# A GNN stack on one core: who multiplies the summed paths by their coefficients, and the order of ScalarE's work in the last stage

## The chip, the cores and the metric

The kernel runs on one core of a Trainium2 chip. The metric is the time of one execution on the device in microseconds (us); lower is better. A core has TensorE (matmuls, "PE" in the profile, its weight loads "PEld"), VectorE ("DVE"), ScalarE ("ACT"), GpSimd ("POOL") and SyncE ("SP", which here issues DMAs). Each engine runs its own list of instructions in order, and they wait for one another by semaphores. A "q" behind an engine's name is its sequencer: it decodes, loads registers and waits, and hands instructions to the engine.

## The reference, cut to what matters

Four graph layers run one after another on 256 nodes x 512 features with 8192 edges: a 7-layer GENConv stack, a 4-block sparse attention stack, a mean-aggregating layer, and a segmented tensor product over edges. The change touches only the last one:

```python
# N_SEG = 16, EXTENT = 32, N_PATHS = 64; x_nodes: 256 x 512, x_edges: 8192 x 512
x1 = x_nodes[src].reshape(-1, N_SEG, EXTENT)
x2 = x_edges.reshape(-1, N_SEG, EXTENT)
i1, i2, i3 = (path_indices[:, 0], path_indices[:, 1], path_indices[:, 2])
contrib = path_coeffs[None, :, None] * x1[:, i1, :] * x2[:, i2, :]
edge_out = jnp.zeros((x2.shape[0], N_SEG, EXTENT)).at[:, i3, :].add(contrib)
out = jnp.zeros((n_nodes, OP_SIZE)).at[dst].add(edge_out.reshape(-1, OP_SIZE))
```

Each edge gets 64 "paths": segment `i1` of its source's features times segment `i2` of its own, times a coefficient, added into segment `i3` of the edge's result. The results are then summed over the edges of each destination node.

## The kernel before, in words

The 8192 edges are 64 tiles of 128. The last stage takes them in five groups of 10, 14, 14, 14 and 12 tiles (`SIZES`), so one VectorE instruction handles one path for a whole group: 128 partitions x (tiles x 32) elements, which is 320, 448 or 384 elements. The groups are called 0 to 4 here.

The 64 paths are treated in two ways.

- 44 of them (`SUMMED`) are "summed paths" or **rows**. For row r VectorE first forms a product with its coefficient into one of four slots of `prod` (line 1333, `scalar_tensor_tensor`: (source * coefficient) * edge), and later adds it into the group's `sums` at segment i3 (line 1323). The addition stands `AHEAD` = 2 rows behind the product, so the order is product r, addition r-1, product r+1, and so on. The slices are found by registers: `load_rows` (line 1317) loads the indices of up to four rows from SBUF into registers, on VectorE's sequencer. Each addition waits until the addition before it has ended, since both may write the same segment.
- 20 of them are five **sets** of four. VectorE forms their products without a coefficient (`set_rows`, line 1342) into `tail` and `prods` by turns, and TensorE sums them over destinations at once (`sum_set`, line 968) into its own accumulator. The coefficients come in at the end: ScalarE copies each accumulator out with its coefficient (line 729, `sums_out`), and TensorE spreads it to its segment (`spread_set`, line 976), for which ScalarE builds placing matrices (`place_rows`, lines 710 and 712).

VectorE's order in a group: set 0, a clearing of part of `sums`, rows 0 to 15, set 1, 7 rows, set 2, 7 rows, set 3, 7 rows, set 4, 7 rows, and the last two additions. `set_rows(s)` waits until TensorE has used the set two before it.

When a group's rows are done, TensorE adds its `sums` over destinations (`sum_group`, line 954) and then takes the next group's sets. Both need 0/1 matrices of destinations, which ScalarE builds with two activations for each tile (`hot`, lines 698 and 700: a square, then a Relu that waits for it). The matrix of a tile of group g goes to the place of that of group g-1, so it waits until TensorE has summed that tile. At the start of each group ScalarE and GpSimd also clear a part of `sums` (lines 704 and 541). In group 4 ScalarE builds the ten placing matrices first and the destination matrices after them.

In the last group TensorE takes set 0, set 1, spread 0, set 2, spread 1, set 3, spread 2, set 4, spread 3, spread 4, and then sums the group. The two additions to `x` (line 1357) and the store follow.

## Time and profile before

| | us |
|---|---|
| median of 3 runs | 954.59 (952.15 to 957.04) |
| the profiled execution: its own time | 958.74 |
| its span, first to last instruction | 956.9 |
| last stage, from VectorE's first set to the end of the span | 616.5 to 956.9 |

The span is some 2 us shorter than the time, since the time also holds what lies around the instructions. The page's shares are over the whole span; what counts here is the last stage, its last 340 us. A row of the timeline begins with the start and the duration of an instruction (or of several merged ones); what stands in brackets is how long the engine was idle before it and who ended that. Neighbouring instructions on an engine overlap a little, so the distance between two starts is shorter than the duration.

### The profile page before, as it was taken

Reading aid. Unit: us, or ns where it says so; the run is one execution under the profiler, and the core shown is the slowest. Engines: PE = TensorE matmul, PEld = TensorE weight load, DVE = VectorE, ACT = ScalarE, POOL = GpSimd, SP = SyncE. Lnnn points to the kernel's source line nnn. Section 1 sums busy time; section 2 is a strip of 40 time slices with the busy share of each in tenths; the row PEclk is TensorE's granted clock in tenths of the full one; section 3 lists DMA queues with packets and bytes.
Section 4 is the critical chain, followed back from the end, with each engine's and each line's share of the span. In section 5 each row is a group of like instructions: output and inputs, shape, how many; then the busy total and the mean of one; then the engine's idle time right before and its main releaser. Section 6 shows DMA issues by size and latency. Waiting matters only on the chain.

```text
span 956.9 us, 10169 instructions
## 1 busy us (share of the span) xinstructions
PE 784.0 (82%) x2802; PEld 500.9 (52%) x2802; DVE 608.1 (64%) x1562; ACT 226.7 (24%) x449; POOL 141.7 (15%) x153
## 2 busy tenths in 40 slices
PE   7287988978984999999999977126887998979998
PEld 3163554554552756766657543124465475565663
DVE  8463665655667353533543633178999999999980
ACT  6321120120221222222221311300420602406300
POOL 5000000000001000000010000720171081240000
PEclk9678999999996999999999999569998999999999
DMA  6703222322232224324333101820341344130000
GB/s 210 257 1 99 99 88 99 99 88 99 99 99 62 88 72 148 120 83 134 113 105 99 55 1 41 316 82 1 154 122 33 154 132 154 34 99 1 0 1 22
DMA packets 35905, 89.97 MB, mean 94 GB/s; under 512 B 3570, under 2 KB 3967, under 8 KB 35231
## 3 DMA queue, kind: packets, MB, share of 16 engines
q1 hardware_dynamic: 30752, 72.81, 22.0%
q0 software_dynamic: 5120, 16.78, 6.0%
q8 instruction: 13, 0.21, 0.1%
q14 instruction: 20, 0.16, 0.1%
HBM read 88.53 MB, written 1.05 MB: 94 GB/s over the span
## 4 chain that ended last, share of the span: by engine, by line
PE 35%; issue 29%; DVE 19%; DVEq 9%; SPq 3%; POOL 2%; DMA 2%; ACT 1%; POOLq 0%; ACTq 0%
PE PS L736 25%; DVE big L1323 6%; DVEq L1317 6%; PE PS L954 4%; DVE tail L1333 4%; PE PS L968 3%; POOL rstd L527 1%; DMA big<-_L_gnn_path_indices_dram 1%; DVE tail L1342 1%; DVE prods L1342 1%; DVEq L1323 1%; POOL big L547 1%; DVEq L1318 1%; PE PS L770 1%; DVE big L1096 1%
## 5 line engine op out<-in xcount | busy, mean ns | idle before, releaser
L1333 DVE SCALAR_TENSOR_TENSOR tail<-big,coef 128x448 f32 (+2 forms) x220 | 139.0, 634 | 1.5 <-issue 1.5
L736 PE MATMUL PS<-big 128*128 128x512 f32 (+1 forms) x368 | 136.2, 523 | 2.9 <-DVE big L1261 1.8
L1323 DVE TENSOR_TENSOR big<-big,tail 128x448 f32 (+2 forms) x220 | 127.0, 577 | 10.8 <-DVE tail L1333 5.1
L736 PEld LDWEIGHTS PS<-big 128*128 128x128 f32 x368 | 67.9, 190 | 65.8 <-issue 62.0
L527 POOL TENSOR_TENSOR rstd<-var,minus_half 128x1 f32<-128x1 f32 x38 | 28.7, 764 | 472.9 <-DVE var L1010 472.9
L547 POOL DMA_INDIRECT big<-h_rows,src_i x64 | 85.0, 1328 | 83.8 <-PE PS L954 60.6
L736 PE MATMUL PS<-hT,big 128*128 128x256 f32 x384 | 84.9, 381 | 4.2 <-ACT hT L648 4.2
L736 PEld LDWEIGHTS PS<-hT,big 128*128 128x128 f32 x384 | 72.3, 190 | 15.5 <-issue 3.9
L954 PE MATMUL PS<-big,hotd_more 128*128 128x512 f32 x176 | 76.3, 592 | 0.0
L1028 DVE TENSOR_TENSOR h<-PS,h 128x512 f32<-128x512 f32 x26 | 17.9, 689 | 79.7 <-PE PS L736 79.7
L968 PE MATMUL PS<-xn,tail 128*128 128x256 f32 x104 | 30.5, 445 | 40.8 <-issue 27.2
L704 ACT ACTIVATE big<-consts 128x3072 f32<-128x3072 f32 x5 | 13.8, 2762 | 201.3 <-DVE big L1323 187.2
L968 PE MATMUL PS<-xn,prods 128*128 128x256 f32 x96 | 31.2, 483 | 32.2 <-DVE prods L1342 32.2
L954 PEld LDWEIGHTS PS<-big,hotd_more 128*128 128x128 f32 x176 | 33.4, 190 | 42.1 <-issue 42.1
L968 PE MATMUL PS<-hotd_more,tail 128*128 128x256 f32 x224 | 54.3, 399 | 0.0
L968 PE MATMUL PS<-hotd_more,prods 128*128 128x256 f32 x216 | 51.6, 395 | 0.0
L736 PE MATMUL PS<-cnt,big 128*128 128x256 f32 x224 | 50.6, 385 | 0.0
L968 PEld LDWEIGHTS PS<-hotd_more,tail 128*128 128x128 f32 x224 | 46.0, 206 | 7.6
L968 PEld LDWEIGHTS PS<-hotd_more,prods 128*128 128x128 f32 x216 | 44.1, 204 | 7.2
L968 PEld LDWEIGHTS PS<-xn,tail 128*128 128x128 f32 x104 | 21.9, 216 | 49.0 <-issue 29.4
L736 PEld LDWEIGHTS PS<-cnt,big 128*128 128x128 f32 x224 | 42.9, 194 | 5.7
L736 PE MATMUL PS<-big,vhid 128*128 128x256 f32 x96 | 28.6, 464 | 18.5 <-DVE vhid L1125 18.5
(184 smaller groups left out, 1067.0 us busy)
## 6 DMA issues: line engine op xcount, KB each, us to landing
big<-in_L_gnn_vn_W_dram SPq DMA_DIRECT2D x12, 1024.0 KB, 5.3
big<-in_edge_attr_dram SPq DMA_DIRECT2D x3, 3584.0 KB, 10.7
big<-in_L_gnn_m_w_dram SPq DMA_DIRECT2D x8, 1024.0 KB, 5.3
big<-in_L_gnn_gcn_W_dram SPq DMA_DIRECT2D x7, 1024.0 KB, 5.3
big<-in_L_gnn_wv_dram SPq DMA_DIRECT2D x4, 1024.0 KB, 5.3
big<-in_L_gnn_wq_dram SPq DMA_DIRECT2D x4, 1024.0 KB, 5.2
big<-in_L_gnn_wk_dram SPq DMA_DIRECT2D x4, 1024.0 KB, 5.4
big<-in_L_gnn_wo_dram SPq DMA_DIRECT2D x4, 1024.0 KB, 5.4
```

Of the source, the lines that this page charges most:

```text
L527: pool.tensor_tensor(rstd[:, t:t + 1], var[:, t:t + 1], minus_half[:, t:t + 1], ALU.pow).then_inc(ln_est, 1)
L547: pool.indirect_dma_start(out=part[SOURCE_AT[g]][:, j, :], out_offset=None, in_=h_rows, in_offset=bass.IndirectOffsetOnAxis(ap=src_i[:, ti ...
L704: act.activation(cut, zero.to_broadcast([P, (ZERO_CUT[1] - ZERO_CUT[0]) * D]), ACT.Copy).then_inc(acc_zero, 1)
L736: return pe.matmul(o, lhsT, rhs, start=start, stop=stop)
L770: ins = pe.transpose(chunks(0)[:, c, t * P:(t + 1) * P], xn[:, t, c * P:(c + 1) * P], ident[:])
L954: ins = pe.matmul(PS[:, t, :], hotd(j)[:, t * P:(t + 1) * P], part[SUM_AT[g]][:, j, :], start=False, stop=True, skip_group_check=True)
L968: ins = pe.matmul(PS[:, 2 + s, 0:N], prods[n % 2][:, j, :], hotd(j), start=False, stop=True, skip_group_check=True)
L1028: link(dve.tensor_tensor(to[:, t, :], PS[:, bank + t, :], to[:, t, :], ALU.add))
L1317: dve.load([r for four in regs[0:n_rows] for r in four], path[0:1, row * 4:(row + n_rows) * 4])
L1323: dve.tensor_tensor(o, o, prod[:, row % RING, 0:n, :], ALU.add)._wait_ge(path_step, g * STEPS + 2 * row + 1).then_inc(path_step, 1)
L1333: dve.scalar_tensor_tensor(out=prod[:, row % RING, 0:n, :], in0=xs[:, :, bass.ds(i1, EXT)], scalar=coef[:, row:row + 1], in1=xe[:, :, bass ...
L1342: ins = dve.tensor_tensor(prods[(g * SETS + s) % 2][:, 0:n, q * EXT:(q + 1) * EXT], xs[:, :, bass.ds(i1, EXT)], xe[:, :, bass.ds(i2, EXT)] ...
```

## The change

VectorE's product of a row loses its coefficient: it becomes a plain `tensor_tensor` multiplication. ScalarE multiplies each product by its coefficient, in place in `prod` (`scale_row`). VectorE's addition of a row stands three rows behind its product now, and product r waits until ScalarE has scaled row r-2. Behind product 43 VectorE waits for the last scaling, loads registers, and makes three additions.

ScalarE's list in a group is laid out anew: clearing, then rows 0 to 43, each one scaling, with the building work spread among them by `built_by`: a "unit" (two activations: one destination matrix, or in group 4 also one placing matrix) after two of three rows, and two units more after rows 16, 23, 30 and 37, as long as there are units left (14 in groups 1 to 3, 22 in group 4, none in group 0, whose matrices are built before). In group 4 the first four copies of set sums stand behind rows 34, 35, 38 and 41. TensorE's spreads 0, 1 and 2 now stand together behind set 3.

```diff
-AHEAD = 2
+AHEAD = 3
+SUM_OUT_AFTER = (34, 35, 38, 41)
 # ScalarE
+            def scale_row(g, row):
+                act.wait_ge(path_step, g * STEPS + row + 1 + max(0, row - AHEAD + 1))
+                at = prod[:, row % RING, 0:SIZES[g], :]
+                act.activation(at, at, ACT.Copy, scale=coef[:, row:row + 1]).then_inc(scaled, 1)
+            def built_by(row):
+                return 2 * row // 3 + sum(2 for s in range(1, SETS) if row > SUMMED_FIRST + SUMMED_PER_SET * (s - 1))
...
-                if g == GROUPS - 1:
-                    act.wait_ge(negcol_set, 1)
-                    place_rows()
-                for j in range(SIZES[g]):
-                    act.wait_ge(tile_summed, min(START[g - 1] + j + 1, START[g]))
-                    hot(g, j)
+                for row in range(SUMMED):
+                    scale_row(g, row)
+                    for i in range(built_by(row), built_by(row + 1)):
+                        if g and i < SIZES[g]:
+                            act.wait_ge(tile_summed, min(START[g - 1] + i + 1, START[g]))
+                            hot(g, i)
+                        if last and SIZES[g] <= i < SIZES[g] + 2 * SETS:
+                            place_row(i - SIZES[g])
+                    if last and row in SUM_OUT_AFTER:
+                        sum_out(SUM_OUT_AFTER.index(row))
+            sum_out(SETS - 1)
 # TensorE
                     sum_set(g, s)
-                    if g == GROUPS - 1 and s:
-                        spread_set(s - 1)
+                    if g == GROUPS - 1 and s == SETS - 2:
+                        for early in range(SETS - 2):
+                            spread_set(early)
+            spread_set(SETS - 2)
             spread_set(SETS - 1)
 # VectorE
                     dve.tensor_tensor(o, o, prod[:, row % RING, 0:n, :], ALU.add)._wait_ge(
-                        path_step, g * STEPS + 2 * row + 1).then_inc(path_step, 1)
+                        path_step, g * STEPS + min(2 * row + AHEAD - 1, SUMMED + row)).then_inc(path_step, 1)
...
-                                dve.scalar_tensor_tensor(
-                                    out=prod[:, row % RING, 0:n, :], in0=xs[:, :, bass.ds(i1, EXT)],
-                                    scalar=coef[:, row:row + 1], in1=xe[:, :, bass.ds(i2, EXT)],
-                                    op0=ALU.mult, op1=ALU.mult).then_inc(path_step, 1)
+                                ins = dve.tensor_tensor(prod[:, row % RING, 0:n, :], xs[:, :, bass.ds(i1, EXT)],
+                                                        xe[:, :, bass.ds(i2, EXT)], ALU.mult)
+                                if row >= AHEAD - 1:
+                                    ins._wait_ge(scaled, g * SUMMED + row - (AHEAD - 2))
+                                ins.then_inc(path_step, 1)
...
+                dve.wait_ge(scaled, (g + 1) * SUMMED)
                 summed_rows(SUMMED, SUMMED + AHEAD)
```

Three places show the new order. First ScalarE in group 4, where before all units stood in one run (L710 and L712 build a placing matrix, L698 and L700 a destination matrix; xn and hotd_more hold the latter):

```order
L704 ACTIVATE big<-consts 128x3072 [waits path_step]
L710 ACTIVATE big<-iota_f,negcol 128x256 [waits negcol_set]
L712 ACTIVATE big<-big,consts 128x256 [waits place_squared]
L710 ACTIVATE big<-iota_f,negcol 128x256
L712 ACTIVATE big<-big,consts 128x256 [waits place_squared]
...
L698 ACTIVATE xn<-iota_f,dst_n 128x256 [waits tile_summed]
L700 ACTIVATE xn<-xn,consts 128x256 [waits hot_squared]
...
L729 ACTIVATE big<-PS,setcoef 128x256 [waits set_used] x5
```

Now, in the same group, from row 14's scaling to row 17's and the unit behind it (L718 is a scaling, L700 and L702 a destination matrix, L711 and L713 a placing matrix):

```order
L718 ACTIVATE tail<-tail,coef 128x384 [waits path_step]
L700 ACTIVATE hotd_more<-iota_f,dst_n 128x256 [waits tile_summed]
L702 ACTIVATE hotd_more<-hotd_more,consts 128x256 [waits hot_squared]
L718 ACTIVATE tail<-tail,coef 128x384 [waits path_step] x2
L700 ACTIVATE hotd_more<-iota_f,dst_n 128x256 [waits tile_summed]
L702 ACTIVATE hotd_more<-hotd_more,consts 128x256 [waits hot_squared]
L700 ACTIVATE hotd_more<-iota_f,dst_n 128x256 [waits tile_summed]
L702 ACTIVATE hotd_more<-hotd_more,consts 128x256 [waits hot_squared]
L711 ACTIVATE big<-iota_f,negcol 128x256
L713 ACTIVATE big<-big,consts 128x256 [waits place_squared]
L718 ACTIVATE tail<-tail,coef 128x384 [waits path_step]
L711 ACTIVATE big<-iota_f,negcol 128x256
```

The "x2" are the scalings of rows 15 and 16; three units stand between the scalings of rows 16 and 17. Groups 1 to 3 have the same order there.

Second, TensorE in group 4 behind set 2, before (L968 sums a set; a second row of it per set, without `set_ready`, is left out; L976 spreads, L954 sums the group):

```order
L968 MATMUL PS<-xn,prods 128x256 [waits hotd_ready,set_ready]
...
L976 MATMUL PS<-big 128x512 [waits sums_out,place_ready]
L976 MATMUL PS<-big 128x512
L968 MATMUL PS<-xn,tail 128x256 [waits hotd_ready,set_ready]
...
L976 MATMUL PS<-big 128x512 [waits sums_out,place_ready]
L976 MATMUL PS<-big 128x512
L976 MATMUL PS<-big 128x512 [waits sums_out,place_ready]
L976 MATMUL PS<-big 128x512
L954 MATMUL PS<-big,xn 128x512 [waits path_step]
```

And now (L988, L996 and L974 are the same three):

```order
L988 MATMUL PS<-xn,prods 128x256 [waits hotd_ready,set_ready]
...
L996 MATMUL PS<-big 128x512 [waits sums_out,place_ready]
L996 MATMUL PS<-big 128x512
L996 MATMUL PS<-big 128x512 [waits sums_out,place_ready]
L996 MATMUL PS<-big 128x512
L996 MATMUL PS<-big 128x512 [waits sums_out,place_ready]
L996 MATMUL PS<-big 128x512
L988 MATMUL PS<-xn,tail 128x256 [waits hotd_ready,set_ready]
```

Between set 3 and set 4 there was one spread (number 2, the first L976 pair shown); now there are three, numbers 0, 1 and 2.

Third, the end of a group on VectorE, before (L1333 is a product, L1323 an addition, L1317 the register load, the ISA rows register arithmetic):

```order
L1323 TENSOR_TENSOR big<-big,tail 128x12x32 [waits path_step]
L1333 ISA
L1333 SCALAR_TENSOR_TENSOR tail<-big,coef 128x384
L1317 TENSOR_LOAD path
L1318 ISA
L1323 TENSOR_TENSOR big<-big,tail 128x12x32 [waits path_step]
L1323 ISA
L1323 TENSOR_TENSOR big<-big,tail 128x12x32 [waits path_step]
```

And now (L1357 is a product, L1345 an addition, L1339 the register load):

```order
L1345 TENSOR_TENSOR big<-big,tail 128x12x32 [waits path_step]
L1357 ISA
L1357 TENSOR_TENSOR tail<-big 128x384 [waits scaled]
L1339 TENSOR_LOAD path [waits scaled]
L1340 ISA
L1345 TENSOR_TENSOR big<-big,tail 128x12x32 [waits path_step]
L1345 ISA
L1345 TENSOR_TENSOR big<-big,tail 128x12x32 [waits path_step]
L1345 ISA
L1345 TENSOR_TENSOR big<-big,tail 128x12x32 [waits path_step]
```

The last register load now waits for ScalarE, and three additions stand behind it where there were two.

## Rows read from the trace of the kernel before

**Rows 1.** Windows, group 1 and group 4: length, busy times, clock.

```profile
core 0: us, PE busy (x) PEld busy (x) DVE busy (x) ACT busy (x) POOL busy (x), PEclk, DMA share, GB/s
676.00:741.00 65.00, 55.38 (x181) 38.07 (x182) 62.45 (x110) 16.74 (x30) 24.14 (x16) 0.89 0.34 114
870.00:932.00 62.00, 60.02 (x196) 38.13 (x196) 55.38 (x109) 24.83 (x50) 1.57 (x1) 0.97 0.00 1
```

**Rows 2.** Timeline, VectorE, group 1: rows in steady state.

```profile
683.51 0.62 DVE L1323 TENSOR_TENSOR big<-big,tail 128x448 f32 x1
684.04 0.68 DVE L1333 SCALAR_TENSOR_TENSOR tail<-big,coef 128x448 f32 x1
684.64 0.62 DVE L1323 TENSOR_TENSOR big<-big,tail 128x448 f32 x1
685.77 0.62 DVE L1323 TENSOR_TENSOR big<-big,tail 128x448 f32 x1
687.00 0.62 DVE L1323 TENSOR_TENSOR big<-big,tail 128x448 f32 x1
```

**Rows 3.** Timeline, start of group 1 and its product 19.

```profile
676.33 2.76 ACT L704 ACTIVATE big<-consts 128x3072 f32<-128x3072 f32 x1 [68.59 <-DVE big L1323]
677.50 2.23 DVE L1342 TENSOR_TENSOR prods<-big 128x448 f32 x4 [1.21 <-issue]
680.73 1.15 DVE L1333 SCALAR_TENSOR_TENSOR tail<-big,coef 128x448 f32 x2
704.67 0.67 DVE L1333 SCALAR_TENSOR_TENSOR tail<-big,coef 128x448 f32 x1
```

**Rows 4.** Timeline, end of group 3 on VectorE, start of group 4.

```profile
867.83 0.68 DVE L1333 SCALAR_TENSOR_TENSOR tail<-big,coef 128x448 f32 x1
868.42 1.28 DVE L1323 TENSOR_TENSOR big<-big,tail 128x448 f32 x2
870.77 1.97 DVE L1342 TENSOR_TENSOR tail<-big 128x384 f32 x4 [1.06 <-issue]
873.72 1.02 DVE L1333 SCALAR_TENSOR_TENSOR tail<-big,coef 128x384 f32 x2
```

**Rows 5.** Groups of instructions from 600 us on: busy us, mean ns of one.

```profile
L1333 DVE SCALAR_TENSOR_TENSOR tail<-big,coef 128x448 f32 x132 | 88.6, 673 | 0.0
L1342 DVE TENSOR_TENSOR prods<-big 128x448 f32 x32 | 17.9, 620 | 3.1 <-issue 2.7
```

**Rows 6.** One group of ScalarE's instructions, whole span.

```profile
L623 ACT ACTIVATE big<-big,consts 128x512 f32<-128x512 f32 x14 | 10.1, 723 | 0.5
```

**Rows 7.** Timeline, ScalarE in group 4: one unit and the next one's start.

```profile
882.75 0.49 ACT L698 ACTIVATE xn<-iota_f,dst_n 128x256 f32<-128x256 f32 x1
883.27 0.51 ACT L700 ACTIVATE xn<-xn,consts 128x256 f32<-128x256 f32 x1
883.68 0.49 ACT L698 ACTIVATE xn<-iota_f,dst_n 128x256 f32<-128x256 f32 x1
```

**Rows 8.** Register loads of line 1317: ns, least, median, most.

```profile
L1317 DVEq TENSOR_LOAD <-path x95: 594/1097/1354, 614.7 to 927.6; - x95
```

**Rows 9.** Timeline, group 4: VectorE's sets and rows, TensorE to the end.

```profile
910.20 1.96 DVE L1342 TENSOR_TENSOR prods<-big 128x384 f32 x4 [0.26 <-issue]
918.05 1.88 PE L976 MATMUL PS<-big 128*128 128x512 f32 x4
919.88 1.96 DVE L1342 TENSOR_TENSOR tail<-big 128x384 f32 x4 [0.26 <-issue]
921.90 2.65 PE L968 MATMUL PS<-xn,tail 128*128 128x256 f32 x8 [1.98 <-DVE tail L1342]
939.17 13.90 PE L954 MATMUL PS<-big,hotd_more 128*128 128x512 f32 x32
953.11 1.29 DVE L1357 TENSOR_TENSOR x<-PS,x 128x512 f32<-128x512 f32 x2 [23.08 <-PE PS L954]
```

**Rows 10.** Windows around TensorE's idle time before set 4.

```profile
922.00:929.00 7.00, 7.00 (x25) 5.87 (x26) 7.00 (x15) 0.00 (x0) 0.00 (x0) 0.76 0.00 0
```

41 lines of the change are left out of this document (22 added, 19 removed).

## The prediction, made before the changed kernel was run

> **What bounds the kernel now.** I read the windows by group first. In groups 1 to 3 VectorE is busy in nearly all of the time (62.45 of 65.00 us in group 1) and TensorE has room; in group 4 TensorE is the full one, 60.02 of 62.00 us, VectorE 55.38 [rows 1]. So up to group 4 a group lasts as long as VectorE takes, and from there the end is set by when TensorE can take set 4: it stands idle for 1.98 us until VectorE has formed it, at 921.84, and from 921.90 it works without a pause up to the last additions at 953.11, 31.2 us later [rows 9]. Nothing before the last stage is touched.
>
> Next, VectorE's steady state. From an addition to the product behind it it is 0.53 us, from the product to the next addition 0.60, so a row takes 1.13; where a register load stands between, additions are 1.23 apart (685.77 to 687.00) [rows 2]. The load itself takes up to 1.10 us on the sequencer [rows 8], so it is hidden but for 0.1, because the sequencer runs about one row ahead. It can't run further, since an addition isn't handed over before the last one has ended: the two additions with nothing between take 1.28 us together, 0.66 apart [rows 4].
>
> ScalarE works for 16.74 us of group 1's 65 [rows 1], so it has room on average. What counts is whether it has it when VectorE waits.
>
> **What is removed.** A product with coefficient takes 673 ns, a plain one of the same 448 elements 620 [rows 5], and four plain ones take 2.23 us, that is 0.54 from start to start [rows 3]. So a product goes from 0.60 to 0.535 on VectorE: 0.065 a row, 44 x 0.065 = 2.9 us in a group, if nothing else paces the row. Behind a register load the load does, so I count two thirds.
>
> **What a scaling costs.** The trace before has no in-place scaling of 448 elements. The nearest rows are the activations from SBUF to SBUF: 0.51 us for 256 elements [rows 7] and 723 ns for 512 [rows 6]; these are the ends of my range. Between them 448 elements give 0.67 us, 384 give 0.62, 320 give 0.56; I take these, since both rows have, as the scaling does, a per-partition operand. Consecutive activations start 0.10 earlier than the last one ends (0.51 long, 0.41 to the next start) [rows 7]. So ScalarE spends 0.57 us a row in groups 1 to 3 and 0.52 in group 4. A unit (square, Relu) takes 0.93 to 0.94 us [rows 7]. The Trainium skill ("ScalarE: Activation LUTs", What ACT_TABLE_LOAD costs) puts an activation at 186 ns, 93 ns more for each per-partition operand and 0.833 ns an element; that is 0.65 us for the scaling, 0.02 less than mine, and by it the sum below would come out at about 976 us; no row here shows which is nearer.
>
> **Rows 0 to 19 of groups 1 to 3.** With a unit behind two rows of three ScalarE needs 0.57 + 0.67 x 0.94 = 1.20 us a row, VectorE only 1.07. Product r waits for scaling r-2, so VectorE can be only two rows ahead. Behind row 16 three units stand in one block, 2.8 us. They follow set 1, in whose 2.23 us ScalarE has nothing to do. Adding up ScalarE's time from the group's start: product 0 starts after 4.4 us (680.73 less 676.33) [rows 3], scaling 0 at 5.1; 18 scalings x 0.57 = 10.3; 13 units x 0.94 = 12.2; idle in set 1 2.2. Scaling 17 ends at 29.8, and product 19, which waits for it, starts at 29.9. Before it started at 704.67, 28.3 after the start [rows 3]: **+1.6 us**. The register load for row 20 stands behind this waiting product and can't be hidden: some 1.4 us with its register arithmetic, of which 0.53 to 1.0 lie beside the product: **+0.7**. ScalarE's wait for `tile_summed` costs nothing here: TensorE needs 1.7 us a tile (32 matmul instructions in 13.90 us, four a tile) [rows 9], ScalarE's units come every 1.8, and later.
>
> **Rows 20 to 43**: 24 x 0.065 = 1.6, two thirds of it: **-1.0**. ScalarE has no units left there, 0.57 against 1.07, so it hides.
>
> **The end of a group.** Before: product 43 starts at 867.83, the last addition ends at 869.70, so 1.87 us [rows 4]. Now: product 0.62, hand-over to ScalarE 0.06 (as TensorE's behind set 4 [rows 9]), scaling 0.67, hand-over 0.06, then the register load and its arithmetic, 1.1 (VectorE's 1.06 us of idle time at a group's start, where it waits for just that [rows 4]), and three additions 0.66 + 0.66 + 0.62. That is 4.45: **+2.6**. Queued behind are the next group's set 0 and TensorE's `sum_group`; both move by it.
>
> Together a group of 14 tiles has 1.6 + 0.7 - 1.0 + 2.6 = +3.9; three of them **+11.7 us**. Group 0 has no units; its rows are shorter than the loads (two plain operations of 320 elements against a load of 1.10 every four rows plus arithmetic), so I count a third of 44 x 0.06, -0.9, and +2.5 for its end: **+1.6**.
>
> **Group 4, up to set 4.** 22 units now, three more at each set. Product 0 comes after 4.0 us [rows 4], so scaling 0 at 4.6. Up to scaling 27: 28 x 0.52 = 14.6, 21 units x 0.94 = 19.7, idle in sets 1 and 2 3.9: 42.8. Product 29 waits for it, then the load (1.4) and set 3 (1.96) and the product itself (0.5) follow: set 3 ends at 46.7 at least, 47.2 with half of the exposed loads. Before it ended at 912.16, 42.4 after 869.73 [rows 4, 9]: +4.8. From there to the end of set 4 it is as long as before (9.7). Set 4 comes **+4.8** later.
>
> **TensorE's new order.** Set 4 stands behind spreads 0, 1 and 2 now, and spread 2 needs the copy that ScalarE makes behind scaling 38, while product 38 stands behind set 4 on VectorE. From the end of set 4: to the start of product 38 1.5, product 0.55, hand-over 0.06, scaling 0.62, copy 0.06 + 0.47 + 0.06, spread 1.7 (1.88 busy [rows 9]): TensorE starts set 4 5.0 us after VectorE has it, where it was 0.06 before: **+4.9**. Set 4, spreads 3 and 4 and the last group then take their 31.2 us as before. VectorE's last addition (seven rows and the longer end, 11 us behind set 4) lies beside TensorE's 15.
>
> **Sum:** 11.7 + 1.6 + 4.8 + 4.9 = 23.0. Against the profiled execution, 958.74, that is 981.7. The median of the runs is 4.15 below that one, so **977.6, say 978 us**. With scalings of 0.51 us some 10 would go (18 x 0.16 less in each of three groups, 28 x 0.11 in the last, of which VectorE's own pace keeps some): 968. With 0.723: 18 x 0.05 x 3 + 28 x 0.1 = 5.5 more: 983. These bound the likeliest case.
>
> **Rivals.**
> (A) Slower still, by the clock: TensorE's idle time lowers it. Behind 1.98 us of idle time the window of set 4 has a mean granted clock of 0.76, a mix of the two levels 1.2 and 2.4 GHz [rows 9, 10]. Now its idle times before sets 3 and 4 are longer. If set 4 ran at the low level throughout, its 24 instructions would take twice 0.216 each, 10.3 us for the 7.0 of before, and spread 2 as much again as it has, 1.7: +5. With long scalings that is 985 to 988. The Trainium skill ("TensorE: Matmul & The Clock Gate", HAM oscillation) says just this: work in bursts with idle gaps between starts cold each time. By it alone the sum would be 983. Against it: the three spreads fill part of the gap.
> (B) ScalarE's work is covered. If a scaling took under 0.44 us of its time (1.07 less 0.63 for units), VectorE would never wait in the rows. Left are the product's gain, -1.9 in a group, -0.5 for a product moved ahead of the first addition, and the end, +2.6: +0.2 x 3; group 0 +1.6; group 4 -2.0 and +4.9. Sum +5.1: 960. For it: on average ScalarE is idle for 48 of 65 us [rows 1]. Against it: 0.51 us for 256 elements.
> (C) Faster: three rows of distance let the sequencer run ahead, and the register loads vanish from VectorE's path. Then groups 1 to 3 get the full 2.9 and 1.0 of load stalls, and the last load is read ahead of its wait, so the end costs only 1.2: -2.7 x 3; group 0 -4 (it has the most load stalls); group 4 -1: -13, 942. It decides at the point where a waiting product no longer stops its sequencer. Against it: additions still wait one for another [rows 4], and the load is a sequencer instruction behind the wait.
> (D) The change doesn't do what it says: a plain product is no quicker here. Against it are 132 and 32 instructions of one shape [rows 5]. It would add 44 x 0.065 x 2/3 x 4 = 7.6: 985.
>
> **How the numbers follow.** Forecast 0.64; A 0.12; B 0.14; C 0.06; D 0.04. I take 0.5% (4.8 us) as what a measurement of this kernel tells from no change. B lies on that edge, half of it on either side. Slower: 0.64 + 0.12 + 0.04 + 0.07 = 0.87; same 0.07; faster 0.06. The range goes from 963, between B and the lower end of the forecast, to 990, with A and D in it.
>
> **What would show it.** Product 19 of group 1 some 30 us behind the group's start, with a wait for ScalarE, and products 17 and 18 without one. At each end of a group some 2.6 us between product 43 and the first of three additions. Groups 1 to 3 lasting 68 us instead of 64 to 65. In group 4 TensorE waiting for ScalarE's copy before spread 2. A scaling of 0.62 to 0.70 us for 448 elements. I am wrong if VectorE's products don't wait for ScalarE behind row 16, if the end of a group is under 3 us, or if TensorE takes set 4 at once.

## The result, and the profile after

| | before | after |
|---|---|---|
| median of 4 runs each, us | 953.87 (952.15 to 957.04) | 975.72 (971.93 to 978.36) |
| span of the profiled execution, us | 956.9 | 974.1 |

The changed kernel takes 1.0222 times as long, with a 95% interval of 1.0178 to 1.0266. The forecast was 978 us, slower; it came out slower, at 975.7.

The lines are L1357 for a product, L1345 for an addition, L1367 for a set's product and L718 for a scaling. By form, from 600 us on (columns: busy us, mean ns | idle before, releaser), in a second profile of the changed kernel:

```profile
L718 ACT ACTIVATE tail<-tail,coef 128x448 f32<-128x448 f32 x132 | 86.0, 662 | 64.9 <-DVE tail L1357 64.9
L1345 DVE TENSOR_TENSOR big<-big,tail 128x448 f32 x132 | 81.9, 620 | 13.2 <-DVE tail L1357 7.2 <-issue 5.8
L1357 DVE TENSOR_TENSOR tail<-big 128x448 f32 x132 | 81.3, 618 | 4.9 <-ACT tail L718 4.9
L718 ACT ACTIVATE tail<-tail,coef 128x384 f32<-128x384 f32 x44 | 25.9, 606 | 14.9 <-DVE tail L1357 14.9
```

A product went from 673 to 618 ns [rows 5] (forecast: 620). A scaling takes 662 ns for 448 elements and 606 for 384 (forecast: 670 and 620). An addition still takes 620 ns, so VectorE's own instructions don't get longer with ScalarE scaling beside them. The change does what it says.

The waits of the last stage in the first profile (us in total, times, longest):

```profile
DVE big L1345 <- DVE tail L1357: 13.9, 24, 1.0
DVE big L1345 <- issue: 11.1, 10, 1.9
DVE tail L1357 <- ACT tail L718: 8.8, 10, 1.7
```

Of 220 products only 10 show a wait for ScalarE. The additions lost more than the products: a register load that isn't ready in time shows as idle time before the addition that stands behind it. In the kernel before, these idle times come to 5.1 us in 10 places, here to 13.9 in 24. Most of them stand behind products that show no wait themselves. In group 1 (scaling 5, product 7 and the addition behind it):

```profile
684.75 0.65 ACT L718 ACTIVATE tail<-tail,coef 128x448 f32<-128x448 f32 x1
685.68 0.62 DVE L1357 TENSOR_TENSOR tail<-big 128x448 f32 x1
686.98 0.63 DVE L1345 TENSOR_TENSOR big<-big,tail 128x448 f32 x1 [0.68 <-DVE tail L1357]
```

Product 7 may start when scaling 5 has ended, at 685.40. That is early enough for the engine, which gets to product 7 at 685.68, but VectorE's sequencer hadn't been able to pass the wait and load the registers of the next four rows before. The same happens at product 11; the version below without any scaling has no idle time at these two places. In group 1 the additions lose 2.4 us in this way, in four places, where they lost 0.5 before.

The timeline of VectorE at product 19 of group 1, which answers to [rows 3]; the group starts at 674.07:

```profile
701.47 0.62 DVE L1357 TENSOR_TENSOR tail<-big 128x448 f32 x1
702.01 0.62 DVE L1345 TENSOR_TENSOR big<-big,tail 128x448 f32 x1
704.06 0.62 DVE L1357 TENSOR_TENSOR tail<-big 128x448 f32 x1 [1.44 <-ACT tail L718]
705.32 0.63 DVE L1345 TENSOR_TENSOR big<-big,tail 128x448 f32 x1 [0.63 <-DVE tail L1357]
705.86 0.62 DVE L1357 TENSOR_TENSOR tail<-big 128x448 f32 x1
```

And ScalarE in the same stretch (L700 and L702 are the two activations of a unit):

```profile
699.98 0.67 ACT L718 ACTIVATE tail<-tail,coef 128x448 f32<-128x448 f32 x1 [2.00 <-DVE tail L1357]
700.56 0.49 ACT L700 ACTIVATE hotd_more<-iota_f,dst_n 128x256 f32<-128x256 f32 x1
701.08 0.51 ACT L702 ACTIVATE hotd_more<-hotd_more,consts 128x256 f32<-128x256 f32 x1
...
702.96 0.51 ACT L702 ACTIVATE hotd_more<-hotd_more,consts 128x256 f32<-128x256 f32 x1
703.38 0.65 ACT L718 ACTIVATE tail<-tail,coef 128x448 f32<-128x448 f32 x1
```

Product 19 starts 0.03 us after scaling 17 ends (703.38 + 0.65). Between scalings 16 and 17 stand the three units, from 700.56 to 703.47. Just before, while VectorE formed set 1, ScalarE was idle for 2.00 us. So it was not short of time; its work stood in the wrong place. The addition behind product 19 starts 1.26 us after it, where the steady distance is 0.53, again because of a register load.

The end of group 3, which answers to [rows 4]:

```profile
874.49 0.62 DVE L1357 TENSOR_TENSOR tail<-big 128x448 f32 x1
877.00 1.94 DVE L1345 TENSOR_TENSOR big<-big,tail 128x448 f32 x3 [1.89 <-issue]
880.01 1.97 DVE L1367 TENSOR_TENSOR tail<-big 128x384 f32 x4 [1.07 <-issue]
```

From product 43 to the end of the last addition it is 4.45 us, where it was 1.87. The 1.89 us hold the wait for the last scaling and the load behind it. They are put down to "issue", not to ScalarE, since the wait is an instruction of the sequencer.

TensorE, from the sum of group 3 (L974) through group 4's sets (L988) and spreads (L996); it answers to [rows 9]:

```profile
878.99 9.73 PE L974 MATMUL PS<-big,xn 128*128 128x512 f32 x16 [3.58 <-DVE big L1345]
...
926.74 3.78 PE L988 MATMUL PS<-xn,prods 128*128 128x256 f32 x8 [5.31 <-DVE prods L1367]
930.32 4.47 PE L988 MATMUL PS<-hotd_more,prods 128*128 128x256 f32 x16
934.63 3.60 PE L996 MATMUL PS<-big 128*128 128x512 f32 x8
939.08 1.95 PE L996 MATMUL PS<-big 128*128 128x512 f32 x4 [0.86 <-ACT big L722]
940.87 1.89 PE L988 MATMUL PS<-xn,tail 128*128 128x256 f32 x8
942.60 3.62 PE L988 MATMUL PS<-hotd_more,tail 128*128 128x256 f32 x16
```

TensorE takes set 4 at 940.87, 61.9 us after the group's start at 878.94; before it was 52.2. It also shows two things that the forecast didn't count: 16 matmuls of the sum take 9.73 us where they took 7.13 before, and set 3 takes 8.05 us (926.74 to 934.79) where a set at full clock takes 5.35 (set 4, 940.87 to 946.22). The windows beside these rows (the column PEclk is the mean granted clock; 1.00 is 2.4 GHz and 0.50 is 1.2):

```profile
core 0: us, PE busy (x) PEld busy (x) DVE busy (x) ACT busy (x) POOL busy (x), PEclk, DMA share, GB/s
926.00:935.00 9.00, 8.43 (x25) 6.84 (x26) 8.49 (x19) 4.95 (x9) 0.00 (x0) 0.65 0.01 3
935.00:973.00 38.00, 34.43 (x92) 17.02 (x90) 10.45 (x21) 5.42 (x10) 0.00 (x0) 1.00 0.04 13
```

These two are from the second profile of the changed kernel, whose set 3 starts at 926.58. At set 3 the clock is mostly at the lower level, and behind it at the full one.

### A comparison that misled at first

By the first two profiles group 0 had become 4.4 us faster (59.7 to 55.4), against a forecast of +1.6. In the first profile of the kernel before, VectorE stood still in group 0 for reasons that no engine's work explains:

```profile
627.14 0.49 DVE L1323 TENSOR_TENSOR big<-big,tail 128x320 f32 x1 [2.70 <-issue]
```

In that stretch the register instructions of VectorE's sequencer take 0.70 us each, where the median is 0.08, while GpSimd issues its gathers. A second profile of each kernel, both on one chip, tells whether the change has to do with it.

> The kernel before again, for group 0 alone. In its first profile some register instructions of VectorE's sequencer took 0.70 us each in group 0, and the group 59.8 us; in the changed kernel there were none and it took 55.4. Theory (it belongs to the execution or the chip, not to the kernel; kernels of one later call had such instructions and those of an earlier call none): the two kernels of this call agree, both with or both without. Rival (the changed order avoids them): before2 has them and lasts about 60 us, after2 none and 55.

> The changed kernel again, for group 0 alone, on the same chip as before2. Theory (execution or chip): as before2, with or without the 0.70 us register instructions, and if with them group 0 lasts about 60 us. Rival (the changed order avoids them): none, and 55 us.

The kernel before took 957.5 us (span 955.7) and the changed one 975.75 (span 973.9), and neither had those long instructions (the longest of L1333 and L1357 takes 0.10 us), though GpSimd issues the same gathers; the same stretch before reads:

```profile
626.89 0.49 DVE L1323 TENSOR_TENSOR big<-big,tail 128x320 f32 x1
627.30 0.55 DVE L1333 SCALAR_TENSOR_TENSOR tail<-big,coef 128x320 f32 x1
```

The same kernel shows them in one execution and not in another, so they are no work of the change. In the profiles of the experiments they were there for all kernels that ran on a chip together, or for none. The medians of the kernel before on these chips fit: 957.99 and 956.75 us where the profiles have them, 953.96 and 954.73 where they have not. What causes them stays open. So between chips the ratios are compared and not the times, and this pair of profiles is the one to compare. A group's length is from the end of its predecessor's last addition to the end of its own; group 4's is to the end of the span:

| us | group 0 | 1 | 2 | 3 | 4 and end | last stage |
|---|---|---|---|---|---|---|
| before, second profile | 54.1 | 64.5 | 64.1 | 64.9 | 87.2 | 334.9 |
| after, second profile | 55.4 | 68.2 | 68.0 | 68.6 | 94.6 | 354.8 |
| difference | +1.3 | +3.7 | +3.9 | +3.7 | +7.4 | +19.9 |
| forecast | +1.6 | +3.9 | +3.9 | +3.9 | +9.7 | +23.0 |

The spans of this pair differ by only 18.2 us, since the last stage starts at 620.81 before and at 619.08 after. Nothing ahead of it was changed; over all the profiles here that start lies between 615.4 and 620.8, so a single execution's time is uncertain by some us for reasons that have nothing to do with the change.

### The profile page after: what moved, and what is told of

Same layout as the page of the kernel before. It is cut to its first block, busy times and chain, and to the rows that moved or that the text cites. A ratio compares the mean times of both kernels' runs of the same rounds, so it can differ in the third digit from the quotient of the medians.

```text
span 974.1 us, 10395 instructions
## 1 busy us (share of the span) xinstructions
PE 791.6 (81%) x2802; PEld 504.2 (52%) x2802; DVE 597.3 (61%) x1562; ACT 353.9 (36%) x669; POOL 127.9 (13%) x153
## 4 chain that ended last, share of the span: by engine, by line
PE 37%; issue 27%; DVE 16%; DVEq 7%; ACT 6%; SPq 3%; POOL 2%; DMA 2%; POOLq 0%; ACTq 0%
PE PS L756 26%; PE PS L974 5%; DVEq L1339 5%; DVE big L1345 5%; PE PS L988 4%; DVE tail L1357 4%; ACT tail L718 2%; POOL rstd L529 1%; DMA big<-_L_gnn_path_indices_dram 1%; DVE tail L1367 1%; DVE prods L1367 1%; DVEq L1340 1%; POOL big L549 1%; PE PS L790 1%; PE PS L846 1%
## 5 line engine op out<-in xcount | busy, mean ns | idle before, releaser
L718 ACT ACTIVATE tail<-tail,coef 128x448 f32<-128x448 f32 (+2 forms) x220 | 136.6, 631 | 116.7 <-DVE tail L1357 116.6
L1345 DVE TENSOR_TENSOR big<-big,tail 128x448 f32 (+2 forms) x220 | 127.7, 580 | 25.7 <-DVE tail L1357 13.9
L1357 DVE TENSOR_TENSOR tail<-big 128x448 f32 (+2 forms) x220 | 126.7, 578 | 8.8 <-ACT tail L718 8.8
L756 PEld LDWEIGHTS PS<-big 128*128 128x128 f32 x368 | 67.9, 190 | 65.9 <-issue 62.0
L549 POOL DMA_INDIRECT big<-h_rows,src_i x64 | 71.2, 1112 | 87.5 <-PE PS L974 64.3
L974 PE MATMUL PS<-big,hotd_more 128*128 128x512 f32 x176 | 76.3, 592 | 0.0
L988 PE MATMUL PS<-xn,tail 128*128 128x256 f32 x104 | 29.4, 432 | 39.2 <-DVE tail L1367 39.2
L988 PE MATMUL PS<-hotd_more,prods 128*128 128x256 f32 x216 | 52.8, 397 | 5.5 <-ACT hotd_more L702 5.5
L988 PE MATMUL PS<-xn,prods 128*128 128x256 f32 x96 | 31.4, 485 | 29.8 <-DVE prods L1367 29.8
L974 PEld LDWEIGHTS PS<-big,hotd_more 128*128 128x128 f32 x176 | 33.4, 190 | 42.1 <-issue 42.1
L974 PE MATMUL PS<-big,xn 128*128 128x512 f32 x80 | 43.6, 707 | 14.0 <-DVE big L1345 14.0
L988 PE MATMUL PS<-hotd_more,tail 128*128 128x256 f32 x224 | 52.2, 388 | 0.0
L988 PEld LDWEIGHTS PS<-hotd_more,prods 128*128 128x128 f32 x216 | 42.5, 200 | 14.3 <-ACT hotd_more L702 8.3
L756 PE MATMUL PS<-big,vhid 128*128 128x256 f32 x96 | 34.3, 536 | 18.6 <-DVE vhid L1147 18.6
L988 PEld LDWEIGHTS PS<-hotd_more,tail 128*128 128x128 f32 x224 | 44.1, 197 | 6.6
L988 PEld LDWEIGHTS PS<-xn,tail 128*128 128x128 f32 x104 | 22.0, 217 | 46.7 <-DVE tail L1367 42.1
```

Source lines behind the costliest of these rows:

```text
L549: pool.indirect_dma_start(out=part[SOURCE_AT[g]][:, j, :], out_offset=None, in_=h_rows, in_offset=bass.IndirectOffsetOnAxis(ap=src_i[:, ti ...
L718: act.activation(at, at, ACT.Copy, scale=coef[:, row:row + 1]).then_inc(scaled, 1)
L756: return pe.matmul(o, lhsT, rhs, start=start, stop=stop)
L974: ins = pe.matmul(PS[:, t, :], hotd(j)[:, t * P:(t + 1) * P], part[SUM_AT[g]][:, j, :], start=False, stop=True, skip_group_check=True)
L988: ins = pe.matmul(PS[:, 2 + s, 0:N], prods[n % 2][:, j, :], hotd(j), start=False, stop=True, skip_group_check=True)
L1345: dve.tensor_tensor(o, o, prod[:, row % RING, 0:n, :], ALU.add)._wait_ge(path_step, g * STEPS + min(2 * row + AHEAD - 1, SUMMED + row)).th ...
```

## The experiments

All ratios are to the kernel before, run on the same chip, with a 95% interval. Group lengths are from the profiles.

### One cost at a time: the units moved

```diff
-  ... sum(2 for s in range(1, SETS) if row > SUMMED_FIRST + SUMMED_PER_SET * (s - 1))
+  ... sum(2 for s in range(1, SETS) if row >= SUMMED_FIRST + SUMMED_PER_SET * (s - 1))
```

The block of extra units now stands behind row 15, that is beside set 1 on VectorE, and likewise one row earlier at the other sets.

> The two extra units stand behind the scalings of rows 15, 22, 29 and 36 instead of 16, 23, 30 and 37, so ScalarE builds them while VectorE forms a set. Theory (the block of units holds back scaling 17, and product 19 behind it): product 19 of groups 1 to 3 starts some 28 us behind the group's start instead of 29.8 to 30.1, these groups last about 66 us instead of 68, set 4 of group 4 ends at about 52.5 us instead of 57.0, and the whole is 8 to 11 us faster than the changed kernel. Rival (the scalings slow VectorE whatever the order, by traffic or by ScalarE's total work): groups 1 to 3 stay at 68 us and the whole within 2 us.

Measured: 969.06 us, ratio 1.0164 (1.0133 to 1.0194). Groups 1 to 3 last 66.3, 67.1 and 66.7. VectorE at product 19 of group 1 (the group starts at 672.95):

```profile
700.89 0.61 DVE L1345 TENSOR_TENSOR big<-big,tail 128x448 f32 x1
701.42 0.61 DVE L1357 TENSOR_TENSOR tail<-big 128x448 f32 x1
702.31 0.62 DVE L1345 TENSOR_TENSOR big<-big,tail 128x448 f32 x1 [0.27 <-DVE tail L1357]
```

Product 19 starts at 28.5, where it was before the change, and shows no wait; the load behind it costs 0.27 instead of 0.63. The mechanism is as forecast. The idle time before additions hardly fell, though: 12.6 us in all instead of 13.9, since the exposed loads of rows 0 to 15 are still there. The whole gained 6.7 us (the kernel before took 953.96 here and 953.87 beside the changed kernel), less than the 8 to 11 expected. Group 2 gave only 1.0, since there VectorE stood idle for 1.25 us before set 2 (it may take the place of set 0 only when TensorE has used that). Group 4 and the end gave 3.1 of it (92.1 instead of 95.2), since in group 4 VectorE's set 3 is still 2.3 us later than before the change and TensorE idles 3.43 us before it.

### One cost at a time: the end of a group

```diff
-                dve.wait_ge(scaled, (g + 1) * SUMMED)
-                summed_rows(SUMMED, SUMMED + AHEAD)
+                for k, (_, _, i3) in enumerate(load_rows(SUMMED, AHEAD)):
+                    if k:
+                        dve.wait_ge(scaled, (g + 1) * SUMMED - AHEAD + 1 + k)
+                    add_product(SUMMED - AHEAD + k, i3)
```

The registers are loaded first, and each addition waits for its own scaling.

> At a group's end the register load stands ahead of the wait, and additions 42 and 43 wait for scalings 42 and 43 each; addition 41 waits for none. Theory (the end costs 4.45 us because the load is serial with the wait for scaling 43): product 43 to the last addition's end falls to about 3.0 us, 1.4 less in each of groups 0 to 3; in group 4 it is hidden, so 5 to 6 us in all. Rival (the wait for the scaling alone costs it, the load is hidden): 4.1 to 4.4 us, under 1.5 us in all.

Measured: 969.5 us, ratio 1.0162 (1.0135 to 1.0189). The end of group 1:

```profile
732.97 0.61 DVE L1357 TENSOR_TENSOR tail<-big 128x448 f32 x1
733.50 1.93 DVE L1345 TENSOR_TENSOR big<-big,tail 128x448 f32 x3
```

The three additions follow with no gap: 2.47 us from product 43 to the end, instead of 4.45 (about 3.0 was expected). Groups 1 to 3 last 66.2, 65.9 and 66.7, each some 2 less. So 2.0 of the +2.6 at a group's end go with the order of load and waits, and 0.6 with the third addition. The edit does two things at once, and no run has them apart: the load stands ahead of the waits, and additions 41 and 42 no longer wait for scaling 43. By the terms of the forecast, an estimate, the first is worth 1.1 us and the second some 0.8.

### TensorE's new order in group 4: the copy, or the whole order?

```diff
-SUM_OUT_AFTER = (34, 35, 38, 41)
+SUM_OUT_AFTER = (34, 35, 36, 41)
```

This takes away only what the forecast names for the term: spread 2's wait for the copy behind scaling 38.

> Only the copy of set 2's sums stands behind row 36 instead of 38, ahead of set 4. By the prediction's term (TensorE gets set 4 4.9 us late because of spread 2's copy) the end would come some 3 to 5 us earlier. By the rival reading of the changed kernel's trace (TensorE waits only 0.86 us for that copy, the rest are spreads that it has to do anyway and that were kept out of its idle time before set 3) it comes about 1 us earlier.

Measured: 975.92 us, ratio 1.0227 (1.0199 to 1.0255); group 4 and the end 94.2, against 95.2. TensorE:

```profile
936.19 5.31 PE L996 MATMUL PS<-big 128*128 128x512 f32 x12
941.34 1.89 PE L988 MATMUL PS<-xn,tail 128*128 128x256 f32 x8
```

All three spreads run in one piece, and set 4 comes only 1.0 us earlier in the group than in the first profile of the changed kernel (60.9 after its start at 880.4), and 0.5 earlier than in the second (61.4). The copy was the last to come, but behind it TensorE was late by itself. The other version moves the spreads to where TensorE is idle, before set 3:

```diff
-SUM_OUT_AFTER = (34, 35, 38, 41)
+SUM_OUT_AFTER = (27, 28, 31, 41)
-                    if g == GROUPS - 1 and s == SETS - 2:
-                        for early in range(SETS - 2):
-                            spread_set(early)
+                    if g == GROUPS - 1 and s == SETS - 3:
+                        spread_set(0)
+                        spread_set(1)
+                    if g == GROUPS - 1 and s == SETS - 2:
+                        spread_set(2)
```

> Copies behind rows 27, 28, 31 and 41; TensorE takes spreads 0 and 1 behind set 2, spread 2 behind set 3. Theory (5.3 us of TensorE's idle time before set 3 are what group 4 loses, and set 3 then runs at a lower clock): spreads 0 and 1 lie in the idle time, set 3 runs at the full clock, TensorE starts set 4 within 0.2 us of its end on VectorE (57.0 us after the group's start, instead of 61.9), and the end comes 3 to 5 us earlier. Rival (VectorE's last addition or the clock sets the end): under 1.5 us.

Measured: 971.79 us, ratio 1.0195 (1.0163 to 1.0227); group 4 and the end 92.2, that is 3.0 and 2.4 less than in the two profiles of the changed kernel. TensorE:

```profile
921.02 3.67 PE L996 MATMUL PS<-big 128*128 128x512 f32 x8 [2.17 <-ACT big L722]
924.53 1.89 PE L988 MATMUL PS<-xn,prods 128*128 128x256 f32 x8
926.25 3.62 PE L988 MATMUL PS<-hotd_more,prods 128*128 128x256 f32 x16
929.71 1.88 PE L996 MATMUL PS<-big 128*128 128x512 f32 x4
933.36 1.99 PE L988 MATMUL PS<-xn,tail 128*128 128x256 f32 x8 [1.77 <-DVE tail L1369]
```

The gap of 5.31 us is mostly filled (2.17 are left), set 3 runs at full clock (5.34 us), and set 4 waits for VectorE again, as before the change. What is left of group 4's loss, 5.0 us, is as much as set 4 comes late on VectorE.

### All three together

> The three repairs together: units built beside the sets, the register load ahead of the last waits, copies and spreads in TensorE's idle time. Theory (three separate costs that add up): groups 1 to 3 last about 64.6 us (68.2 less 1.6 less 2.0), group 0 53.8, group 4 and the end about 85, so the time is about 947 us, some 1% under the kernel before, of which most is group 0. Rival (the costs hide one another, ScalarE's total work in rows 3 to 20 is the floor): groups 1 to 3 stay above 66 us and the time above 958.

Measured: 960.31 us against 957.99 for the kernel before on this chip, ratio 1.0031 (1.0011 to 1.0050). The 947 us expected were missed. Groups 1 to 3 came as expected, but group 4 and the end took 2 us more, and group 0 took 59.8 instead of 53.8: the expectation had compared with a kernel before that has the long register instructions, and not counted them here, where this profile has them too. In all, the last stage took 340.0 us where the expected lengths add up to 332.6; the other 6 us lie outside these lengths and stay unexplained.

Groups 1 to 3 last 64.3, 64.0 and 64.8, and group 4 and the end 87.1: each as before the change. So the three costs account for nearly all of the loss (0.3 of 2.2% is left), but the plain product gives nothing back even then. Rows 0 to 15 still take longer: from product 3 to product 15 of group 1 it is 14.9 us (6.8 to 21.7), against 13.8 before (7.8 to 21.5). ScalarE, with its units between the scalings, holds the waits of products 7 and 11 until shortly before they start, and the loads behind them stay exposed: 2.0 us of idle time before additions in this group, 0.5 before the change. The end of a group is 0.6 longer.

### Is it the length of a scaling?

```diff
-                act.activation(at, at, ACT.Copy, scale=coef[:, row:row + 1]).then_inc(scaled, 1)
+                act.activation(at, at, ACT.Copy, scale=2.0).then_inc(scaled, 1)
```

This kernel leaves the coefficients of the summed paths out of the result.

> The changed kernel with a constant 2.0 in place of the coefficient operand of the scaling; it leaves the coefficients of the summed paths out of the result. By the Trainium skill (ScalarE: Activation LUTs, What ACT_TABLE_LOAD costs) an activation is 93 ns shorter without a per-partition operand. Theory (ScalarE's own pace sets rows 3 to 19 and the sets of group 4): scalings of 448 elements take 0.56 to 0.58 us instead of 0.65 to 0.67, product 19 of groups 1 to 3 starts 1 to 1.7 us earlier, the whole is 5 to 8 us faster. Rival (the waits come from hand-over times, not from the scaling's length): under 2 us.

Measured: 977.34 us, ratio 1.0209 (1.0159 to 1.0258): no gain. Scalings did get shorter:

```profile
L718 ACT ACTIVATE tail<-tail 128x448 f32<-128x448 f32 x132 | 74.7, 572 | 74.2 <-DVE tail L1357 71.1 <-issue 2.5 <-DVE big L1345 0.6
```

572 ns instead of 662, and product 19 starts at 29.1, 28.9 and 29.2 instead of 30. The expectation failed all the same. In group 3 VectorE stands idle 1.3 us before set 2, because it waits until TensorE has used set 0. That is late, since TensorE's sum of group 2 starts slowly (27.3 us for the whole sum, 24.3 in the kernel before). There the wait moved from ScalarE to TensorE. Groups 1 to 3 last 67.2, 67.0 and 68.7, that is 1.0, 1.0 and -0.1 us less than in the changed kernel. These 2 us are within the spread of the runs (975.65 to 981.24). The wait of product 19 fell only from 1.44 to 1.25 us. The ratio, 1.0209 against 1.0222, says the same (the time itself holds the long register instructions, with 60.7 us for group 0). So 91 ns less for a scaling take away about a tenth of the loss at most.

### How much could the change give at all?

In the kernel before, only the product is made plain; the coefficients of the summed paths are left out.

```diff
-                                dve.scalar_tensor_tensor(..., scalar=coef[:, row:row + 1], ..., op0=ALU.mult, op1=ALU.mult)
+                                dve.tensor_tensor(..., ALU.mult)
```

> The kernel before with the plain product on VectorE and no scaling anywhere; it leaves the coefficients of the summed paths out. This is all that the change could give. Theory (0.065 us a row, a third of it lost behind register loads): groups 1 to 3 last 62.6 instead of 64.5 us, the whole is 7 to 10 us faster than before. Rival (the register loads pace the rows): under 3 us. Group 0: if its 4.4 us less in the changed kernel come with the plain product, it lasts 55 to 56 us here, otherwise 59.

Measured: 951.95 us, ratio 0.9939 (0.9910 to 0.9967), 6 us where 7 to 10 were expected. Groups 1 to 3 last 62.9, 62.8 and 63.5, some 1.4 less than before, where the forecast's share for this (two thirds of 2.9) is 1.9. So with ScalarE's part free, the plain product is worth 0.6%. That is the ceiling for the product. It isn't quite that of the whole change: the additions still stand two rows behind here. Three rows bring product 3 of group 1 forward, from 7.7 us after the group's start here to 6.8 in the changed kernel, and cost 0.6 at the group's end.

### TensorE's clock: kept busy before a sum

```diff
                     sum_set(g, s)
+                    if g < GROUPS - 1 and s == SETS - 1:
+                        keep_busy(7, 8)
```

Eight matmuls on an unused part of the accumulator (16 rows in the trace, two for each) fill the gap before each sum.

> The changed kernel with eight more matmuls (identity times a constant, into a bank that nobody reads) behind set 4 of groups 0 to 3, in TensorE's idle time of 3.5 us before each group's sum. Theory (that idle time lowers the granted clock, so that a sum of 14 tiles takes 27.0 us instead of 24.3): the sums take 24.3 to 24.6 us again, set 0 of group 4 ends 2.5 us earlier, and set 2 of group 4, which waits for it, comes 0.5 to 1.5 us earlier; groups 1 to 3 stay at 68 us, and the whole is 0 to 2 us faster. Rival (the slow sums hold VectorE in every group): groups 1 to 3 fall to 66 us or less.

Measured: 974.11 us, ratio 1.0210 (1.0173 to 1.0247). TensorE at the sum of group 3, to be read beside 878.99 above:

```profile
874.16 3.62 PE L756 MATMUL PS<-iota_f,ident 128*128 128x256 f32 x16
877.65 7.13 PE L974 MATMUL PS<-big,xn 128*128 128x512 f32 x16
```

The first 16 matmuls take 7.13 us in all three groups, instead of 9.73 to 9.91 in the first profile of the changed kernel. But groups 1 to 3 last as long as without this edit (68.2, 67.9, 68.6), and group 4 and the end take 94.7, against 95.2 and 94.6 in the two profiles of the changed kernel. The slow start of the sums is real; in the changed kernel as it is, at most some half a microsecond hangs on it.

### A version built on the findings

Rows 0 to 15 keep the coefficient on VectorE, ScalarE builds all units there and scales only rows 16 to 43; the end of a group is that of the second experiment, and TensorE has the order of before with `SUM_OUT_AFTER = (22, 28, 32, 41)`.

```diff
+OWN = SUMMED_FIRST
+                for j in range(SIZES[g]): hot(g, j)
+                for row in range(OWN, SUMMED): scale_row(g, row)
+                                if row < OWN: dve.scalar_tensor_tensor(...)
+                    if g == GROUPS - 1 and s:
+                        spread_set(s - 1)
```

> Rows 0 to 15 keep the coefficient in VectorE's product, as before the change; only rows 16 to 43 are scaled by ScalarE, which builds all its units first, as before. Copies behind rows 22, 28, 32 and 41, spreads in the old order behind each set, register load ahead of the last waits. Theory: no product waits for a unit; a group gains 28 rows x 0.065 x 2/3 = 1.2 us and 0.5 for the product ahead, and loses 0.6 at its end, so groups 1 to 3 last 63 to 63.8 us, and the whole takes 944 to 949 us. Rival (scalings in place slow VectorE's own instructions): groups 1 to 3 at 65 us or more.

Measured: 956.46 us, ratio 0.9980 (0.9952 to 1.0007): no difference from before, where 944 to 949 us were expected. As in the version with all three, group 0 has the long register instructions (59.1 us), which that expectation didn't count; this explains a part of the difference. Groups 1 to 3 last 62.7, 65.1 and 63.8, so groups 1 and 3 came as expected. In group 1 the idle time before additions is down to 0.2 us, from 2.0 with all three repairs: with no scaling in rows 0 to 15, the loads there are hidden again. Group 2 has a wait of its own (VectorE, us in total, times, longest; L1363 is a product here and L720 a scaling):

```profile
DVE tail L1363 <- ACT tail L720: 1.7, 1, 1.7
```

There ScalarE's last unit waited for TensorE's sum of group 1, whose first 16 matmuls took 8.83 us, and scaling 16 behind it came late. The same kernel with four matmuls to keep TensorE busy before each sum tests that:

> e8_mixed with four more matmuls into an unread bank behind set 4 of groups 0 to 3. In e8_mixed group 2 lasted 65.1 us, since product 18 waited 1.7 us for scaling 16, which stood behind a unit that waited for TensorE's sum, and that sum ran at a lower granted clock (26.0 us). Theory (the clock is what delays it): the sum of group 2 takes 24.3 us, the wait goes, group 2 lasts 63 to 63.5 us, and the whole is 0.4 to 0.8% faster than the kernel before. Rival (units paced by tile_summed hold scaling 16 whatever the clock): group 2 at 65 us, no difference from the kernel before.

Measured: 959.5 us, ratio 1.0027 (1.0002 to 1.0052). The wait is gone, and group 2 lasts 63.4 instead of 65.1, as expected; the whole is not faster, against the expectation. In the two profiles, which both have the long register instructions, the last stage is 1.2 us shorter with the four matmuls (335.6 us against 336.8), but it starts 1.5 us later, at 619.89 against 618.44. They ran on two chips, and of the ratios, 0.9980 and 1.0027, the worse one belongs to the version with the shorter stage; why stays open. No version that computes the whole result is clearly faster than the kernel before.

## Why the prediction was right

**Rows 0 to 19 of groups 1 to 3: right.** Product 19 was forecast 29.9 us after the group's start; it starts at 30.0, 29.8 and 30.1. Products 17 and 18 don't wait. Moving the units removes the wait, which shows that the block of three is the cause. The load behind it costs 0.63 in the idle time (forecast 0.7), so that product 20 starts 2.3 us later than before (31.8 against 29.5), as the two terms say. One cost there has no term in the forecast: the loads exposed at products 3, 7 and 11, 1.8 us of idle time in group 1 where it was 0.5. It doesn't add to the sum, because up to product 19 the forecast goes by ScalarE's pace, and ScalarE is the slower one for most of the way: followed back from 694 us, the chain of work lies on ScalarE from 692.5 us back to 683. But it is where the gain of the plain product goes in rows 0 to 15: with all three repairs it is still there, and with no scaling in these rows it is gone.

**Rows 20 to 43: right.** Products and additions are 0.53 to 0.54 apart. From product 20 to product 43 of group 1 it is 31.9 us where it was 33.1: -1.2, forecast -1.0.

**The end of a group: right.** 4.45 us forecast and measured. The chain is hand-over, scaling, load, additions. The second experiment shows that 2.0 of it go with the order of the load and the waits.

**Group 0:** +1.3, forecast +1.6.

**Group 4 up to set 4: the size is right, in part by luck.** Set 4 ends 56.5 and 57.0 us after the group's start in the two profiles, 52.1 before: +4.4 and +4.9, forecast +4.8. The forecast counts 21 units up to scaling 27; there are 22 in the list, and scaling 27 ends 44.2 us after the group's start in the first profile, not 42.8. What the forecast puts behind it (load 1.4, product 0.5, and half of the exposed loads) is too long by about as much. Products 19 and 26, behind the blocks of units, wait 1.67 us each; product 29, which the forecast names, shows no wait.

**TensorE's new order: the size holds, one link of its cause is short.** TensorE starts set 4 4.96 us after VectorE has it (forecast 5.0; VectorE's row is below), and the last thing that it waited for is the copy, as the forecast says. But the forecast follows only that chain. A second one, TensorE's own work, ends 0.86 us earlier: set 3 at the lower clock, 8.05 us, and three spreads where there was one. That is why taking the copy's wait away gives 0.5 to 1.0 us of the 4.9, and moving the spreads 2.4 to 3.0. VectorE's set 4 in the first profile, which ends at 935.91:

```profile
933.94 1.97 DVE L1367 TENSOR_TENSOR tail<-big 128x384 f32 x4 [0.39 <-issue]
```

**Set 4 at full clock: the term that was mis-sized.** The forecast leaves 31.2 us from there to the last addition; it is 29.4 (940.87 to 970.29). Before, set 4 took 7.14 us behind 1.98 us of idle time, in a window with a mean clock of 0.76 [rows 10]; now spreads run right ahead of it and it takes 5.35, in a window with 1.00. That is -1.8. (Whether it takes the spreads for that isn't shown: in the version with the spreads moved, set 4 took 5.45 us behind 1.77 us of idle time.) So the term is off by 1.8, and group 4 comes to +9.7 - 1.8 = +7.9, where the first profile has 8.0 (95.2 less 87.2). Of the 3.1 us by which the forecast's sum is too high against the second pair, this is the largest part.

**The whole: nearer than the parts, by luck.** The parts of the second pair add up to 3.1 us less than forecast, while 978 is only 2.3 us from the 975.7 measured. The medians differ by 21.9 us, the spans of the second pair by 18.2: where the last stage starts varies by more than the forecast missed.

**A row misread.** The forecast says that a register load takes up to 1.10 us; by [rows 8] that is the median, and the longest takes 1.35. It uses 1.10 for one load, so no term changes.

**The rivals.** (A), the clock, was expected to slow set 4 and spread 2; it doesn't. Its mechanism is there at other places: set 3 of group 4, and most of the sums of groups 1 to 3, before which TensorE's idle time has grown from 1.1 or 1.3 to some 3.5 us. The latter costs next to nothing while VectorE sets the pace. The Trainium skill's rule ("TensorE: Matmul & The Clock Gate", HAM oscillation), that bursts behind long idle gaps start cold each time, holds for five of the eight sums of groups 0 to 3 in the two profiles of the changed kernel, counted from the row of the first 16 matmuls: 9.73 to 9.91 us five times, 7.13 three times, behind gaps of 3.41 to 3.62 us in all eight. So it says what to look for, not what happens each time. (B), covered work, is refuted by product 19, which waits 1.44 us. (C), loads that vanish, fails where it was said to decide: the product that waits does stop its sequencer, as the exposed load behind it shows. (D) is refuted by the 618 ns.

## What to carry to other kernels

Work that moves to an engine with much idle time has to stand at the right place in that engine's order; here three helper tasks between two scalings cost 1 to 2 us a group more than one row earlier. Load registers and do other sequencer work ahead of a wait, not behind it; an engine that shows no wait can still lose time there, when its sequencer gets past the wait only shortly before. Before moving an operation, measure the ceiling by leaving it out: 6 us (0.6%) was all that the plain product could give, and the three new costs, each taken away alone, were 7, 6 and 4 us.

## What the runs showed of the hardware

- TensorE's clock after an idle time isn't set by its length alone. In the second profile of the changed kernel the sums of groups 2 and 3 read:

```profile
810.69 9.87 PE L974 MATMUL PS<-big,xn 128*128 128x512 f32 x16 [3.44 <-DVE big L1345]
...
879.31 7.13 PE L974 MATMUL PS<-big,xn 128*128 128x512 f32 x16 [3.62 <-DVE big L1345]
```

 The longer gap is followed by the full clock. Behind gaps of 1.1 to 1.3 us, in both profiles of the kernel before, these 16 matmuls took 7.13 us; behind 3.00 us, at the sum of group 0, 8.83. Behind 2.08 us they took 7.13 at the sum of group 2 with the units moved, and 8.83 at that of group 1 with the constant scale. The mean granted clock from 811 to 820 us, at the slow sum above, is 0.71, and from 879.3 to 889, at the other, 1.00. What else decides stays open.
- A per-partition scale costs an activation 91 ns at 448 elements (662 or 663 against 572), 91 at 384 (606 against 515) and 91 at 320 (561 against 470). The Trainium skill ("ScalarE: Activation LUTs", What ACT_TABLE_LOAD costs) puts it at 93.
- A register load behind a wait isn't hidden, even where the engine shows no wait: 0.68 us of idle time behind products 7 and 11 of group 1, 0.63 behind product 19, and a part of the 1.89 us at a group's end. With the load ahead of the waits there was no idle time at the end.
- VectorE's register instructions took 0.70 us each in one stretch of some executions. Group 0 of the kernel before lasted 59.7 us with them and 54.1 in an execution without.
